# Whole 32-row bands for the scores of a full self attention, with two PSUM banks for maxima and two bank pairs for exponents of 1024 columns

## The reference

```python
def attention(x, w_qkv, b_qkv, w_o, b_o):
    B, T, D = x.shape                       # 4, 512, 128
    dh = D // N_HEADS                       # 128 // 16 = 8
    qkv = x @ w_qkv + b_qkv
    q, k, v = jnp.split(qkv, 3, axis=-1)
    ...
    scores = jnp.einsum('bqhd,bkhd->bhqk', q, k) / jnp.sqrt(jnp.float32(dh)).astype(x.dtype)
    probs = jax.nn.softmax(scores, axis=-1)
    ctx = jnp.einsum('bhqk,bkhd->bqhd', probs, v).reshape(B, T, D)
    return ctx @ w_o + b_o
```

## Time and profile before

| | us |
|---|---|
| median of 3 runs (2345.46 to 2348.4) | 2346.39 |
| the profiled execution's own time | 2343.91 |
| span of its trace | 2342.2 |
| the stage's lead, 576.8 to 601 | 24.2 |
| its main part, 604 to 1081 (14 steps) | 477 |
| its end, 1081 to 1141 | 60 |

### The profile page before, as it was taken

How to read it: one execution, slowest core, us unless ns; L and a number is a source line. 1 busy time by engine, 2 the same in 40 slices (tenths; PEclk the granted TensorE clock), 3 DMA queues, 4 the chain that set the end, 5 groups by cost and what they waited for, 6 DMA issues and landing times. The chain is left out here.

```text
span 2342.2 us, 31089 instructions
## 1 busy us (share of the span) xinstructions
PE 2015.3 (86%) x9958; PEld 1033.7 (44%) x9958; DVE 1270.1 (54%) x3981; ACT 1020.0 (44%) x2074; POOL 143.0 (6%) x228
## 2 busy tenths in 40 slices
PE   3288874865999999999799977999999998998997
PEld 2144442543322222222377753445454545665664
DVE  7398875645433333333233337776766673674445
ACT  3288871650232232233243425776767673332221
POOL 2000000003000000000000001000000000330000
PEclk7599995985555555555599987999999999898999
DMA  2533202400000000000100011000000000000000
GB/s 57 79 45 37 23 0 46 60 15 0 1 1 1 1 1 0 1 1 1 28 19 19 18 36 37 1 1 1 1 1 1 1 1 1 2 1 18 17 20 25
DMA packets 46252, 36.27 MB, mean 15 GB/s; under 512 B 11732, under 2 KB 42681, under 8 KB 46137
## 3 DMA queue, kind: packets, MB, share of 16 engines
q1 hardware_dynamic: 46137, 34.80, 8.4%
HBM read 28.86 MB, written 5.77 MB: 15 GB/s over the span
## 5 line engine op out<-in xcount | busy, mean ns | idle before, releaser
L765 DVE TENSOR_REDUCE c_NM<-ps_s 128x1 f32<-128x512 f32 x256 | 169.6, 687 | 327.3 <-PE ps_s L587 327.3
L587 PE MATMUL ps_s<-c_KG,c_QG 8*128 8x512 f32 x512 | 307.5, 1092 | 0.8 <-DVE c_NM L765 0.8
L604 PE MATMUL ps_t<-c_QG,c_KG 9*128 9x512 f32 x340 | 269.7, 1092 | 1.3 <-ACT c_PT L707 1.3
L707 ACT ACTIVATE c_PT<-ps_t 128x512 f32<-128x512 f32 x170 | 99.8, 596 | 247.7 <-PE ps_t L604 151.0
L1771 ACT ACTIVATE d_PR<-d_PR,d_NM 128x512 f32<-128x512 f32 x256 | 183.8, 718 | 32.8 <-DVE d_NM L1842 32.8
L1780 ACT ACTIVATE d_PT<-ps_t 128x512 f32<-128x512 f32 x256 | 150.5, 589 | 105.7 <-PE ps_t L1696 105.7
L2582 DVE SCALAR_TENSOR_TENSOR X<-ps_t,GATE,X 128x128 f32<-128x128 f32 x272 | 76.7, 344 | 184.5 <-PE ps_t L2507 184.4
L604 PE MATMUL ps_s<-c_QG,c_KG 9*128 9x512 f32 x172 | 171.0, 1093 | 2.6 <-DMA c_QG<-c_NMT 2.0
L1842 DVE CUSTOM_DVE_ANT_0 d_PR<-ps_s,d_BH 128x512 f32<-128x512 f32 x256 | 165.4, 684 | 0.3 <-PE ps_s L1687 0.2
L993 ACT ACTIVATE a_PR<-a_PR,a_NM 128x128 f32<-128x128 f32 (+3 forms) x256 | 129.8, 555 | 79.0 <-DVE a_NM L974 79.0
L903 PE MATMUL ps_t<-ident,a_PR 128*128 128x128 f32 x640 | 115.4, 289 | 47.1 <-ACT a_PT L917 38.1
(11 more groups left out here) (339 smaller groups left out, 3251.1 us busy)
## 6 DMA issues: line engine op xcount, KB each, us to landing
QX<-split_parts SPq DMA_DIRECT2D x72, 128.0 KB
KX<-split_parts SPq DMA_DIRECT2D x36, 128.0 KB
f_W<-in_L_ffn_w SPq DMA_DIRECT2D x16, 256.0 KB, 3.1
split_parts<-a_PARTS SPq DMA_DIRECT2D x8, 384.0 KB, 11.0
g_W<-in_L_ffn_w SPq DMA_DIRECT2D x24, 128.0 KB, 2.2
split_parts<-b_PARTS SPq DMA_DIRECT2D x4, 384.0 KB, 10.3
X<-in_x SPq DMA_DIRECT2D x4, 256.0 KB
c_QG<-c_NMT SPq DMA_DIRECT2D x64, 2.0 KB
```

The lines of the kernel that those rows point to most:

```text
L587: nc.tensor.matmul(MBANKS[m % 3], QG[head(j, HD8), u % 3, qt * P:(qt + 1) * P], KG[head(j, HD8), u % 3, :], start=True, stop=True).then_in ...
L604: nc.tensor.matmul(KBANKS[m % 3], KG[head(j, HD8 + 1), t % 3, kt * P:(kt + 1) * P], QG[head(j, HD8 + 1), t % 3, :], start=True, stop=True) ...
L765: nc.vector.tensor_reduce(NM[:, u % 2, j, qt:qt + 1], MBANKS[m % 3], AX.X, ALU.max, negate=True).then_inc(s_max, 1)
```

## The change

S and K contract whole bands of 32 rows instead of 8 and 9. S gets two banks instead of three, and waits for the maximum of the tile two before. K gets four banks as two pairs. Only an even tile waits, for the exponent of the pair two pairs before, and ACT takes one exponent of 128 x 1024 for two tiles.

```diff
-    MBANKS = [c.ps_s[:, i, :] for i in range(3)]
-    KBANKS = [c.ps_s[:, 3, :], c.ps_t[:, 0, :], c.ps_t[:, 1, :]]
+    MBANKS = [c.ps_s[:, i, :] for i in range(2)]
+    KPAIRS = [c.ps_s[:, 2:4, :], c.ps_t[:, :, :]]
...
-                    if m >= 3:
-                        pe.wait_ge(s_max, m - 2)
-                    nc.tensor.matmul(MBANKS[m % 3], QG[head(j, HD8), u % 3, qt * P:(qt + 1) * P], KG[head(j, HD8), u % 3, :],
+                    if m >= 2:
+                        pe.wait_ge(s_max, m - 1)
+                    nc.tensor.matmul(MBANKS[m % 2], QG[head(j, CW), u % 3, qt * P:(qt + 1) * P], KG[head(j, CW), u % 3, :],
                                      start=True, stop=True).then_inc(s_m, 1)
...
-                    if m >= 3:
-                        pe.wait_ge(s_exp, m - 2)
-                    nc.tensor.matmul(KBANKS[m % 3], KG[head(j, HD8 + 1), t % 3, kt * P:(kt + 1) * P],
-                                     QG[head(j, HD8 + 1), t % 3, :], start=True, stop=True).then_inc(s_st, 1)
+                    if m % 2 == 0 and m >= 4:
+                        pe.wait_ge(s_exp, m // 2 - 1)
+                    nc.tensor.matmul(KPAIRS[m // 2 % 2][:, m % 2, :], KG[head(j, CW), t % 3, kt * P:(kt + 1) * P],
+                                     QG[head(j, CW), t % 3, :], start=True, stop=True).then_inc(s_st, 1)
...
-                    pe.wait_ge(s_exp, GH * (w + 1))
+                    pe.wait_ge(s_exp, GH // 2 * (w + 1))
...
-                    t, i = divmod(m, TILES)
-                    w, j = m // GH, (i % GH + 2) % GH
+                    w, j = m // GH, (m % GH + 1) % GH
                     act.wait_ge(s_st, m + 1)
-                    if i % GH == 0 and w >= PTS:
+                    if j == 2 and w >= PTS:
                         act.wait_ge(s_pv, w - PTS + 1)
-                    nc.scalar.activation(PT[:, w % PTS, j, :], KBANKS[m % 3], ACT.Exp).then_inc(s_exp, 1)
+                    nc.scalar.activation(PT[:, w % PTS, j:j + 2, :], KPAIRS[m // 2 % 2], ACT.Exp).then_inc(s_exp, 1)
...
-                    exp(m)
+                    if m % 2:
+                        exp(m)
...
-                    nc.vector.tensor_reduce(NM[:, u % 2, j, qt:qt + 1], MBANKS[m % 3], AX.X, ALU.max,
+                    nc.vector.tensor_reduce(NM[:, u % 2, j, qt:qt + 1], MBANKS[m % 2], AX.X, ALU.max,
                                             negate=True).then_inc(s_max, 1)
```

## The result

The changed kernel takes 2168.44 us (median of 4 runs, 2161.6 to 2172.89). The kernel before took 2345.93 us beside it, so the ratio is 0.9242 with an interval of 0.9214 to 0.9269. The profiled execution of the changed kernel took 2172.89 us, with a span of 2171.1.

What follows compares the result with a forecast made beforehand. PE was taken to bound the main part, 96% busy at a clock of 0.52. The terms, −123 main part, +11 lead and −13 end, sum to −125, giving 2221 us (ratio 0.947), range 2190 to 2285.

Steps and rivals of the forecast that it cites:

- What bounds, and why the clock rises: Main part: PE, 96% busy at clock 0.52, sets the pace; rows an instruction uses, zeros included, lift the clock.
- Main part: Stretch from the first K to the V two blocks before S runs out: 14 steps, 477 to 354 us, −123.
- The weight: Main part: 0.85 of the time at clock 1.00, a choice, giving a step of 25.3 us.
- a fall behind the turn: Maxima's transpose, once a step: PE waits some 1.5 us, dropping the clock about every second step; block 5.9 at 1.00.
- The blocks at 1.00: Main part: four kinds of block costed at the high clock, together a step of 23.9 us.
- plain: Main-part block of four tiles without extra work: 4.79 us at 1.00, 7.33 at 0.50, against 6.73 before.
- projection: Main-part block with a projection, two per step: 6.5 us at 1.00, 10.6 at 0.50, against 9.60 before.
- The step at 0.50: Main part at the low clock with the new banks: 37.8 us a step, 529 us for 14, against 34.1 before.
- End: Last stretch, mostly K alone: four banks let all four heads run at once, 3.9 us per block for 6.7; −13 us.
- Lead: First S to first K: two banks need 12 rounds instead of 8, 34.2 us, +11, with no higher clock expected.
- Exponents: ACT: 1.03 us per pair with exponents of 1024, 0 to 0.1 saved, none of it on the main part's path.
- the case with the clock up throughout: Main part all at 1.00: 335 us, −142, total 2192 to 2202 us; the forecast's far end, within its 0.73 chance.

Runs made afterwards that it cites:

- e1: Kernel before with only the rows of S and K raised to 32, keeping three banks each and exponents of 512: 2125.28 us, ratio 0.9049.
- e2: Changed kernel's banks and paired exponents, but S and K on 8 and 9 rows as before: 2394.18 us, ratio 1.0196.
- e3: Changed kernel with 16 rows of each band instead of 32 in S and K: 2391.1 us, ratio 1.0186.
- e7: Changed kernel with its four K banks used one by one and exponents of 512 columns instead of paired 1024: 2167.25 us, ratio 0.9242.
- e6: e1 with S also taking the K banks, six in all, while it runs alone in the lead: 2114.22 us, ratio 0.9028.
- e8: e6 with K also taking the three banks of S in the end, once S has finished: 2111.77 us, ratio 0.8991.

## Why the prediction was off

The direction and the mechanism were right, and two terms of the sum were mis-sized, both the same way.

**What bounds, and why the clock rises: right.** The rows that an instruction uses, rows of zeros included, decide here, as read from the earlier trace rows. e1 shows it with nothing else changed, and e2 shows that the banks alone leave the clock where it was. No run tells whether the rows of the weights' loads or those of the matmuls count, since each edit changes both. The Trainium skill, page "TensorE: Matmul & The Clock Gate", section "What's actually happening", has the gate follow how busy the PE has been and names no rows. The runs disagree: in e3 PE is busy for 475.73 of 518.1 us, 92%, at 0.51, and in the changed kernel for 87% at 0.96.

**Main part: −123 predicted, −155 measured.** The step that failed has two parts.

- *The weight.* I chose 0.85 of the time at 1.00. PEclk is 0.96, which is 0.92 of the time. With that, a step is 1 / (0.92/23.9 + 0.08/37.8) = 24.6 us, and 14 are 344 instead of 354: −10. The mechanism that I had named, a fall behind the turn in every second step, came in 4 of 14 and makes half of the time at 0.50. The other half is the start of the main part, which I had not thought of. And 0.85 didn't follow from my own mechanism: seven falls of the size measured are 24 of 354 us, a share of 0.93.
- *The blocks at 1.00.* The step was 23.9 us and measured 22.3: plain 4.79 against 4.55, projection 6.5 against 6.07, turn 5.9 against 5.63, tile 13 with 5.0 against 4.55. I shortened a round at 0.50 by its two passes, 0.85 us, and it lost 0.95: 2.01 became 1.06, and the 2.11 from S0's load to the first reduction became 1.16 (939.96 to 941.12). The 0.10 fits the load, which takes 0.28 us in the earlier trace rows and 0.18 in the block above, and which I had left as it was. A plain block has two such rounds and a block with a projection four. The one sample of the high clock, 1.27 us in the earlier trace rows, didn't show it: its load starts at 791.90 and takes 0.28 us, and the clock is at 0.50 up to 792.0. With 22.3 and the share of 0.92 a step is 23.05 and 14 are 323, where 321.3 was measured. So the other −22 is here.

The step at 0.50 held within 2%: 519.5 us for 14 in e2, where I had 529. Of its blocks, those with a projection were put at 10.6 and take 10.74. By my own rows it is 9.60 − 3.71 + 2.85 + 2.01 = 10.75, since V follows S3 by a whole round.

**End: −13 predicted, −28 measured.** I costed it at 0.50, though K alone was to run there on 32 rows with V on 128, which is just what I said lifts the clock. It ran at 1.00 with blocks of 2.3 to 4.2 us with K alone. e2 has the end at 0.50 with the same banks, 54.8 us: 5.4 less than before instead of the 13 that I gave to the four K banks, and e1 has 35.4 with the old ones. I had five blocks get 2.8 us shorter. In e2 two of the six with K alone do (6.62 to 3.89 and 7.67 to 4.93 us). A third stops at 5.67, since its V waits for ACT's copy of the last context, a wait that I left out:

```profile
1175.22 1.94 PE L616 MATMUL ps_v<-c_PT,c_VG 128*32 128x512 f32 x8 [1.48 <-ACT c_CT L718]
```

So most of the gain of the end is the clock's, and the banks bring about 3 to 5 us.

**Lead: +11 predicted, +10.8 measured.** I expected no higher clock here, and it stayed at 0.50 with S alone on 32 rows, PE busy for 33.66 of 38.40 us, and for 24.90 of 27.60 in e1. So whole bands alone don't lift the clock, and what does must be more than the rows of one instruction. S comes round every 2.85 us with two banks, at 0.50, as two loads of the lead show:

```profile
582.14 1.09 PEld L587 LDWEIGHTS ps_s<-c_KG,c_QG 32*128 32x128 f32 x4 [2.35 <-DVE c_NM L765]
...
584.99 1.09 PEld L587 LDWEIGHTS ps_s<-c_KG,c_QG 32*128 32x128 f32 x4 [1.76 <-DVE c_NM L765]
```

**Exponents: right.** 1025 ns against 1.03 us, and hidden, which e7 shows by its equal time.

**The price of the third bank.** e1 against the changed kernel gives it at the high clock: 0.59 us per plain block, 38 us in the main part, 11 in the lead and −3 in the end, 46 by the stretches and 43 by the medians. At the low clock it is 43.4, 10.8 and −5.4, or 49 by the stretches (e2 against before, whose medians differ by 48). It depends little on the clock, since what the block waits for is DVE's 1.29 us of two maxima, and DVE doesn't speed up.

**The range.** Its low end, 2190, was the case with the clock up throughout and my block lengths. With the measured lengths that case would be 14 x 22.3 = 312 for the main part, and with the end at its right clock 2343.9 − 165 + 11 − 28 + 2.5 = 2164 us in all, 4 below the median measured. I bounded the unknown share of the clock but put no bounds on the block lengths, which rested on one sample and on halving, and none on the end's clock.

## What to carry to other kernels

Where TensorE is busy nearly all of the time and PEclk stands at 0.50, look at the rows that its matmuls use before looking for a wait: padding a short contraction with rows of zeros that are already in memory cost nothing here and took 9.5% off the whole kernel. It wasn't enough everywhere: the lead, with S alone, stayed at 0.50 with two and with three banks. After such a change, cost each stretch anew at the new clock, the tail as well, and take block lengths from rows well inside a stretch at that clock. Two changes that come together should be priced apart: here the rows alone are worth 221 us, and the deal of the banks that came with them gives 43 back.

## What the runs showed of the hardware

- In the main part the granted clock goes with the rows of S and K, and rows of zeros count: 8 and 9 rows 0.51 or 0.52, 16 rows 0.51, 24 rows 0.85, 32 rows 0.96 or 0.97, all at much the same busy share of PE (87 to 96%). I had not expected a doubling from 8 to 16 to do nothing at all.
- The rows of one instruction don't decide alone. With 32 rows and S alone the lead is at 0.50 with two or three banks (PE busy 88 and 90%) and at 0.68 with six, and the first 13.7 us of the changed kernel's main part are at 0.50 too.
- Where two kinds of matmul alternate, both count: 32 rows with 9 gives 0.55 on the mean, changes from step to step (37.7, 29.8 and 34.1 us), and spreads the runs over 61 us.
- How the chip weighs rows against waiting isn't settled. The runs show the stretches, and the fall behind the turn in 4 of 14 steps came without a difference in the program that I could name. With three banks for S (e1, e6, e8) no step has the fall.
